# Attention of a small transformer stack: value and output weights folded per head, probabilities turned on VectorE, products on four row groups

## The reference

```python
def attn_layer(x, Wqkv, qs, ksc, Wo):          # x: 16 x 256 x 128; 16 heads of 64; float32
    q, k, v = jnp.split(x @ Wqkv, 3, -1)       # each to (b, head, token, 64)
    q = l2norm(q) * qs; k = l2norm(k) * ksc
    q = q * cos * scale + rotate_half(q) * sin * scale
    k = k * cos * inv + rotate_half(k) * sin * inv
    out = local_attention(q, k, v)             # windows of 32 queries, 64 keys each: its own and the one before
    return out.transpose(0, 2, 1, 3).reshape(b, n, INNER) @ Wo

for i in range(6):
    x = attn_layer(shift_tokens(x), Wqkv[i], q_scale[i], k_scale[i], Wo[i]) + x
    x = ffn_layer(shift_tokens(x), ln_g[i], ln_b[i], W1[i], b1[i], W2[i], b2[i]) + x
```

## Time and profile before

| | us |
|---|---|
| median of 3 runs | 3451.17 (3447.96 to 3452.07) |
| the profiled execution | 3446.72 |
| its span | 3444.9 |
| PE busy, share of the span | 96% |
| ACT, DVE, POOL busy, shares | 79%, 71%, 42% |
| mean share of the 16 DMA engines, q1 | 52.5% |

### The profile page before, as it was taken

One profiled execution on the slowest core, in us unless ns is written; L12 is line 12 of the kernel. 1 busy time (PEld: TensorE's weight loads), 2 busy tenths in 40 slices (PEclk: granted clock), 3 DMA queues, 4 the chain that ended last, 5 costly groups with the idle time before them and its releaser, 6 DMA issues.

```text
span 3444.9 us, 152307 instructions
## 1 busy us (share of the span) xinstructions
PE 3317.0 (96%) x63036; PEld 2464.0 (72%) x63228; DVE 2439.2 (71%) x5141; ACT 2709.1 (79%) x9033; POOL 1444.9 (42%) x1276
## 2 busy tenths in 40 slices
PE   6789999999999999999999999999999999999997
PEld 4457777777777777777777777777777777777775
DVE  5667777777777777777777777777777777777774
ACT  5667887878788787778787887878878787878876
POOL 2244443544444354444354444444434354444431
PEclk9999999999999999999999999999999999999999
DMA  2045555555655555555555555565565556455553
GB/s 73 1 109 130 134 122 127 134 132 121 145 117 124 132 134 131 125 134 119 126 140 120 135 129 131 119 145 118 124 137 119 131 132 140 113 129 126 117 135 83
DMA packets 360553, 421.42 MB, mean 122 GB/s; under 512 B 51571, under 2 KB 265094, under 8 KB 359094
## 3 DMA queue, kind: packets, MB, share of 16 engines
q1 hardware_dynamic: 359862, 411.67, 52.5%
HBM read 19.30 MB, written 2.10 MB: 6 GB/s over the span
## 4 chain that ended last, share of the span: by engine, by line
PE 71%; POOL 17%; issue 4%; DVE 2%; ACT 1%; DMA 0%; SPq 0%; POOLq 0%; DVEq 0%
PE ring_ps L1227 16%; POOL qs L610 12%; PE out_ps L1319 12%; PE out_ps L1329 10%; PE ring_ps L1272 8%; PE small_ps L1238 6%; PE score_ps L1290 5%; PE ring_ps L1301 4%; PE ring_ps L1365 4%; POOL probs L594 3%; DVE prod L986 2%; PE ring_ps L1262 2%; PE out_ps L1343 2%; PE score_ps L1282 1%; PE small_ps L1246 1%
## 5 line engine op out<-in xcount | busy, mean ns | idle before, releaser
L767 ACT ACTIVATE probs<-score_ps,neg_max,rq 128x64 f32<-128x64 f32 x3072 | 1200.5, 421 | 94.6 <-DVE neg_max L1024 93.4
L986 DVE TENSOR_TENSOR prod<-ring_ps,tables 128x512 f32<-128x512 f32 x1536 | 957.7, 681 | 288.8 <-PE ring_ps L1227 255.9
L610 POOL TENSOR_TENSOR ks<-prod 128x1024 f32<-128x1024 f32 x192 | 452.7, 2358 | 861.2 <-DVE prod L986 861.2
L1227 PE MATMUL ring_ps<-xs,wqk 128*128 128x256 f32 x3072 | 768.4, 388 | 17.9 <-issue 12.8
L767 ACT ACTIVATION_READ_ACCUMULATOR probs<-score_ps,neg_max,rq 128x1 f32 x3072 | 679.0, 221 | 0.0
L723 ACT ACTIVATE square<-ring_ps,biases 128x512 f32<-128x512 f32 x768 | 517.8, 688 | 198.8 <-DVE prod L986 197.0
L1227 PEld LDWEIGHTS ring_ps<-xs,wqk 128*128 128x128 f32 x3072 | 570.6, 191 | 107.9 <-issue 20.3
L594 POOL TENSOR_TENSOR probs<-probs,inv_sums 128x512 f32<-128x512 f32 x384 | 400.8, 1044 | 581.2 <-DVE inv_sums L1038 581.1
L610 POOL TENSOR_TENSOR qs<-prod 128x1024 f32<-128x1024 f32 x192 | 453.7, 2363 | 382.8 <-DVE prod L986 382.8
L1319 PEld LDWEIGHTS out_ps<-pt,v 64*64 64x64 f32 x24576 | 395.3, 135 | 113.7 <-issue 111.5
L756 ACT ACTIVATE att_t<-out_ps 128x512 f32<-128x512 f32 x384 | 217.3, 592 | 295.6 <-PE out_ps L1319 295.5
(11 more groups left out here) (182 smaller groups left out, 3791.5 us busy)
## 6 DMA issues: line engine op xcount, KB each, us to landing
v<-vs SPq DMA_DIRECT2D x1344, 128.0 KB
qt<-qs SPq DMA_DIRECT2D x768, 128.0 KB
kt<-ks SPq DMA_DIRECT2D x768, 128.0 KB
v<-vs SPq DMA_DIRECT2D x192, 64.0 KB
wqk<-in_L_ffn_Wqkv SPq DMA_DIRECT2D x6, 1024.0 KB, 5.1
wv<-in_L_ffn_Wqkv SPq DMA_DIRECT2D x6, 512.0 KB, 5.7
wo<-in_L_ffn_Wo SPq DMA_DIRECT2D x6, 512.0 KB
out_dram<-ks SPq DMA_DIRECT2D x16, 128.0 KB, 1.9
```

The costliest lines, as they stand in the source:

```text
L610: pool.tensor_tensor(dst, prod_a[p % 2], prod_b[p % 2], ALU.add).then_inc(rot_ready, 1)
L767: last = nc.scalar.activation(probs[i][:, j, e, :], score_ps[e][:, KEYS * j:KEYS * (j + 1)], ACT.Exp, bias=neg_max[:, h:h + 1], scale=rq[p ...
L986: last = V.tensor_tensor((prod_b if a else prod_a)[p % 2][:, f, :] .rearrange("p (u c) -> p u c", u=2), bank[:, :].rearrange("p (u c) -> p ...
L1227: last = mm(bank_of(s)[:, TOKENS * f:TOKENS * (f + 1)], wqk[:, n, 2 * c + f, a, :], xs[:, WINDOW:PADDED], start=True, stop=True)
```

## The change

- The values are not computed any more. For each head, the value weights (128 x 64) and its output weights (64 x 128) are multiplied on the chip into one 128 x 128 matrix, `fold`. That is done for layer 0 before the first batch, in four parts, and for the layer after in four parts (MW on PE, MC on ACT) in the batches 8 to 11 of a layer. The steps V, VC, the moves MV and the load of `wv` go.
- In place of the values the shifted input itself is turned (XT, four transposes on PE; XC, a copy on DVE) into `x2`, in two versions 32 tokens apart, for the keys of the window before and of the own window.
- The probabilities are turned in blocks of 32 x 32 by `V.transpose` on DVE (DT, four instructions of 128 x 512), in place of T and TC.
- PV0 and PV1: eight products each, with 32 contracted rows, 128 output rows and 512 columns (16 heads by 32 queries); the four windows of a tile lie on four row groups and write to four banks. The step before had 64 products in two halves, on 64 x 64.
- The output of PV is 16 heads by 128 channels, so that WO has 16 products in place of 8. It is cut in four steps, WO0 to WO3. The copies OC are eight of 128 x 512, five on ACT and three on DVE.
- The banks are five, given by a table `BANK_OF`, and `bank_free` waits for whoever last used each bank. The orders of all engines are new; S0 stands first on PE. MQ and MK stay, behind the same semaphores, as do all steps not named here.
- `wv_turned` is an input laid out by the host in place of the columns of V.

```diff
 PE_ORDER = """
-PA0 PB0 PA1 S00 S01 PB1 BI WO PA2 NK CEN PB2 VAR PA3 PB3 TK UP0 UP1 S10 S11 V0 UP2 T00 TU NQ KN0 PAD V1 PV00 KN1
-TQ T01 V2 DN T10 PV01 V3 T11 PV10 PV11
+S0 PB0 PA0 PB1 WO0 PA1 WO1 PA2 PB2 PA3 NK S1 TK WO2 PB3 BI WO3 TU XT CEN KN1 VAR NQ KN0 UP0 UP1 TQ UP2 PV0 DN PV1
+MW
 """
 DVE_ORDER = """
-XS RA0 RB0 RA1 M0 RB1 BI XA XB AR00 RA2 RB2 CK XG RB3 RA3 H0 M1 AR01 H1 TC00 UC H2 KM0 CQ VC1 KM1 AR10 TC01 X
-AR11 TC10 VC3 TC11
+XS M0 RA0 RB0 RB1 AR00 RA1 RA2 RB2 RA3 CK DT00 M1 RB3 BI XA XB AR10 AR01 UC XC KM1 XG KM0 CQ DT01 AR11 H0 H1 DT11
+DT10 H2 OC00 OC03 X OC12
 """
 ACT_ORDER = """
-QA0 QB0 QA1 E00 QB1 E01 E02 SQ QA2 LN E03 QB2 RTK LG G0 QB3 QA3 G1 VC0 G2 LE E10 E11 E12 E13 VC2 OC00 OC01 OC10
-RTQ OC11
+E00 E01 QA0 QB0 QB1 E02 QA1 E03 QA2 QB2 RTK QA3 E10 E11 E12 SQ QB3 LN E13 LG G0 G1 G2 LE OC02 OC01 RTQ OC11 OC13
+OC10 MC
 """
 POOL_ORDER = """
-AD0 AD1 TB0 AD2 AN00 AD3 RK AN01 TB1 AN10 AN11
+AD0 AN00 AD1 TB0 AD2 RK AD3 TB1 AN01 AN11 AN10
 """
 SP_ORDER = """
-LK MQ MK LV LL MV
+LK MQ MK LL LM
+"""
+BANK_OF = """
+PB0:3 PA0:4 PB1:2 WO0:0 PA1:1 PA2:3 PB2:2 PA3:4 PB3:2 TU:1 XT:3 CEN:4 KN1:0 KN0:1 UP0:3 UP1:0 UP2:2 PV0:4,0,3,1
+DN:2 PV1:1,0,3,4 BI:4 MW:3,4
 """
...
-            def move_v():
-                for e in range(2):
-                    for m in range(WPT):
-                        src = vs[WINDOW * m:WINDOW * (m + 1), :, e, :]
-                        for half in range(2):
-                            row_ = KEYS * e + WINDOW * half
-                            w0_ = m + 1 - half
-                            tiles = TILES if w0_ < WPT else TILES - 1
-                            sp.dma_start(v2[row_:row_ + WINDOW, w0_:w0_ + WPT * (tiles - 1) + 1:WPT, :],
-                                         src[:, 0:tiles, :]).then_inc(v_moved, 16)
...
+            def make_fold(layer, part, banks):
+                if part == 0:
+                    pe.wait_ge(fold_landed, 32 * (layer + 1))
+                for j in range(2):
+                    for e in range(2):
+                        side = slice(64 * e, 64 * e + 64)
+                        last = mm(banks[e][:, DIM * j:DIM * (j + 1)], wv_turned[side, 2 * part + j, :],
+                                  wo[side, 2 * part + j, :], start=True, stop=True, skip_group_check=True)
+                last.then_inc(fold_made, 1)
...
+                if kind == "XT":
+                    pe.wait_ge(xs_ready, at(g, 1, 1))
                     bank_free(g, s)
...
+                    for k in range(2):
+                        for i in range(TILES):
+                            col = P * i + WINDOW * k
+                            last = pe.transpose(bank_of(s)[:, P * (TILES * k + i):P * (TILES * k + i + 1)],
+                                                xs[:, col:col + P], ident[:, :])
+                    last.then_inc(x_turned, 1)
...
+                if kind == "PV":
+                    i = s[1]
+                    pe.wait_ge(x2_ready, at(g, 1, 1))
                     bank_free(g, s)
...
+                    last_turn = max(rank(DVE_ORDER, ("DT", i, c), "DT") for c in range(2))
+                    pe.wait_ge(turn_ready, at(g, 2 * TILES, last_turn + 1))
+                    for k in range(2):
                         for w in range(WPT):
+                            rows = slice(WINDOW * w, WINDOW * (w + 1))
+                            last = mm(bank_of(s, w), x2[rows, parity, k, i, :],
+                                      turned[rows, i, :, WINDOW * k:WINDOW * (k + 1)],
+                                      start=(k == 0), stop=(k == 1))
+                    last.then_inc(pv_ready, 1)
                 if kind == "WO":
...
+                    part = s[1]
+                    if part == 0:
+                        bank_free(g, s)
+                        for order in (ACT_ORDER, DVE_ORDER):
+                            copied(pe, copies(order)[-1], g)
+                        if b == 0:
+                            pe.wait_ge(fold_ready, 2 * M_PARTS * (layer + 1))
+                    for h in range(WO_PARTS * part, WO_PARTS * (part + 1)):
+                        last = mm(bank_of(("WO", 0)), fold[layer % 2][:, h, :], att_t[:, h, :], start=(h == 0),
+                                  stop=(h == HEADS - 1))
+                    if part == WO_PARTS - 1:
+                        last.then_inc(wo_ready, 1)
+                if kind == "MW" and runs(s, g):
+                    bank_free(g, s)
+                    make_fold(layer + 1, b - M_FIRST, [bank_of(s, e) for e in range(2)])
                 if kind == "BI" and b == 0:
                     pe.wait_ge(late_landed, layer * (16 * late_per_layer) + 16 * late_per_layer)
...
+                if kind == "DT":
                     i, c = s[1], s[2]
...
+                    dve.wait_ge(scaled, at(g, 2 * TILES, rank(POOL_ORDER, ("AN", i, c), "AN") + 1))
+                    if g > 0:
+                        dve.wait_ge(pv_ready, at(g - 1, TILES, rank(PE_ORDER, ("PV", i), "PV") + 1))
+                    V.transpose(turned[:, i, 8 * c:8 * c + 8, :].rearrange("p h k -> p (h k)"),
+                                probs[i][:, 4 * c:4 * c + 4, :, :].rearrange("p j e k -> p (j e k)")
+                                ).then_inc(turn_ready, 1)
+                if kind == "OC":
+                    i, w = s[1], s[2]
+                    dve.wait_ge(pv_ready, at(g, TILES, rank(PE_ORDER, ("PV", i), "PV") + 1))
+                    dve.wait_ge(wo_ready, at(g, 1))
+                    V.tensor_copy(att_t[:, :, P * i + WINDOW * w:P * i + WINDOW * (w + 1)],
+                                  bank_of(("PV", i), w).rearrange("p (h q) -> p h q", q=WINDOW)
+                                  ).then_inc(o_dve, 1)
```

More of the change, by code:

```diff
@@ L111, in rank, with runs, copies @@
     return [x for x in order if x[0] in kinds].index(s)
-RING = [s for s in PE_ORDER if s[0] in ("PA", "PB", "TU", "KN", "V", "T", "DN", "PAD")]
-BANKS = 3
-assert len(RING) % BANKS == 0
+def runs(s, g):
+    b, layer = g % BATCH, g // BATCH
+    if s[0] == "BI":
+        return b == 0
+    if s[0] in ("MW", "MC"):
+        return layer < DEPTH - 1 and M_FIRST <= b < M_FIRST + M_PARTS
+    return True
+def copies(order):
+    return [x for x in order if x[0] == "OC"]
+BANKS = 5
+HALF_BANK = ("WO", "CEN", "DN", "TU", "BI", "MW")
 def build(nc, t):
@@ L149, in build @@
         wqk = sb("wqk", [P, 2, QUADS, 2, P])
-        wv = sb("wv", [P, INNER])
-        wo = [sb(f"wo{i}", [P, PAIRS, DIM]) for i in range(2)]
+        wv_turned = sb("wv_turned", [P, PAIRS, DIM])
+        wo = sb("wo", [P, PAIRS, DIM])
+        fold = [sb(f"fold{i}", [P, HEADS, DIM]) for i in range(2)]
         w1 = [sb(f"w1_{i}", [P, 2 * DIM_INNER]) for i in range(2)]
@@ L353, in walk, with users_before @@
                         step(s, g, b, g % 2, layer)
-        def users_before(seq, s, g, banks):
-            k = seq.index(s) - banks
-            while k >= -2 * len(seq):
-                u = seq[k % len(seq)]
-                gu = g + (stage(u) - stage(s) + k // len(seq))
-                if 0 <= gu < DEPTH * BATCH:
-                    yield u, gu
-                k -= banks
-        def user_before(seq, s, g, banks):
-            return next((x for x in users_before(seq, s, g, banks) if x[0] != ("PAD",)), (None, None))
+        def users_before(s, g):
+            need = set(BANK_OF[s])
+            period, k = g - stage(s), PE_ORDER.index(s)
+            while need and period >= -1:
+                k -= 1
+                if k < 0:
+                    k, period = len(PE_ORDER) - 1, period - 1
+                u = PE_ORDER[k]
+                gu = period + stage(u)
+                if u in BANK_OF and 0 <= gu < DEPTH * BATCH and runs(u, gu):
+                    for i, bank in enumerate(BANK_OF[u]):
+                        if bank in need:
+                            need.remove(bank)
+                            yield u, i, gu
         def walk_first(order, step):
@@ L712, in first_step, with copy_fold @@
                                          bias=mod[:, b, 3:4], scale=mod[:, b, 4:5]).then_inc(lh[1], 1)
+            def copy_fold(layer, part, banks):
+                for e in range(2):
+                    heads = fold[layer % 2][:, :, :].rearrange("p (j e) n -> p j e n", e=2)
+                    nc.scalar.activation(heads[:, 2 * part:2 * part + 2, e, :],
+                                         banks[e].rearrange("p (j n) -> p j n", n=DIM), ACT.Copy
+                                         ).then_inc(fold_ready, 1)
             walk_first(ACT_FIRST, first_step)
+            for part in range(M_PARTS):
+                act.wait_ge(fold_made, part + 1)
+                copy_fold(0, part, [bank_ps[n][:, 0:TOKENS] for n in ((0, 1), (2, 4))[part % 2]])
             def step(s, g, b, parity, layer):
@@ L1216, in step @@
+            first_proj = next(x for x in PE_ORDER if x[0] in ("PA", "PB"))
+            first_kn = next(x for x in PE_ORDER if x[0] == "KN")
```

(1 more changed line is left out.)

336 lines of the change are left out of this document (156 added, 180 removed).

## The result

The changed kernel takes 3556.31 us (median of 4 runs, 3550.04 to 3558.44), the kernel before 3451.62 beside it: 1.0302 times as long, 95% interval 1.0284 to 1.032. The profiled execution has a span of 3548.2. So it is slower by 3.0%, where 2.6% was forecast (3540).

What follows compares the result with a forecast made beforehand. The prediction took PE to bound the kernel before, and the chain of q's and k's moves to bound it after: 96 x 34.3 + 245 = 3538, plus 2 outside the span, 3540 us (+2.6%), range 3410 to 3650.

Steps and rivals of the forecast that it cites:

- The deciding chain: From k's landing through scores, projections and POOL's last sum to SP's moves of q and k: 34.3 us a batch.
- the walk: Step-by-step sum along the move chain, using durations from the trace before: POOL's last sum ends at 20.6, period 34.3 us.
- One sign: On PE ahead of S0's scores: idle time put down to k's DMA, 1.5 to 3 us a period.
- The second chain: From ACT's exponentials to the second gelu, then PV0, bank copies, PV1, scores and masks: 32.4 us a batch.
- E00: First part of the exponentials on ACT, where the second chain starts; from it to the second gelu 23.1 us was walked.
- TensorE's sum: PE's busy time per batch: 33.1 - 10.1 + 3.5 + 0.5 + 3.7 + 0.1 = 30.8 us.
- Row groups: In PV0 and PV1 on PE: four row groups run at once, 1.8 us a step, 3.7 for both.
- the third rival: Chain of ACT, DVE and PV takes over, transposes at 1.35, row groups half overlapping: period about 36, 3700 us; chance 0.10.
- The fourth rival: Row groups on PE don't overlap: both PV steps 6.9 us, period 42.6, 4330 us; chance 0.05.
- The fold: 20 small steps in all, under 0.2 us a period, plus four before the first batch, some 5 us once.
- The moves are shorter: SP's 16 issues of q and k take 10.3 us with V off the queue: period 33.0, 3415 to 3450; chance 0.20.
- PE stays the bound: TensorE takes the whole gain, the moves costing no wait: 30.8 x 96 + 260 = 3215 us; chance 0.10.

Runs made afterwards that it cites:

- e1: The changed kernel with four of the eight DMAs of every move of q left out behind the first batch: 3488.70 us, ratio 1.0129.
- e2: The changed kernel with one swap in PE_ORDER, PB3 before WO2, everything computed: 3491.63 us, ratio 1.0133.
- e4: The changed kernel with four of the eight DMAs of every move of q and of k left out behind the first batch: 3487.61 us, ratio 1.0126.
- e9: The changed kernel, orders laid anew, 28 steps allowed one period earlier, first scores ahead of PV1, everything computed: 3348.87 us, ratio 0.9712.
- e6: The changed kernel with PB3 before WO2, MW between UP0 and UP1 in other banks, and MC ahead of the first gelu: 3454.78 us, ratio 1.0015.
- e5: The changed kernel with all steps kept, the five engine orders and the bank table laid afresh: 3666.80 us, ratio 1.0626.

## Why the prediction was right, and where it was off

**The deciding chain: right, in its place and its size.** AD3 ended 20.85 behind the scores (median; 20.6 in the walk), MQ followed by 0.1, MK stood directly behind MQ. From the first issue to the landing it took 13.2 (median; 12.2 to 14.1), where the walk had 11.6 + 1.9 = 13.5. The two terms are not separate: in the mean the whole took 13.0 behind the 38 bursts whose 16 issues took under 10.7, and 13.1 behind the 56 longer ones, since k often landed later behind a short burst. One of them, SP's rows:

```profile
1844.62 5.11 SPq L503 DMA_DIRECT2D qt<-qs  x8
1849.85 5.10 SPq L503 DMA_DIRECT2D kt<-ks  x8
```

The last issue ends at 1854.95; the scores start at 1858.00, 3.05 later. In 65 of 94 batches the scores start 0.04 behind k's landing; 20 of the 29 others are those with a fold step. e1, e2 and e4 show that the moves did decide: each of three ways to shorten that chain gives the same 65 to 69 us. One sign failed all the same: the idle time ahead of S0 was to be 1.5 to 3 us a batch and was 1.0 where there was any, and in total no more than PV's. PE's waits in total thus put the two chains level; that the scores start right behind k's landing, and the experiments, decide between them.

**The second chain: right in its path, mis-sized.** Walked at 32.4, measured at 33.2. Its terms: E00 to G1 23.4 for 23.1; PV0 to PV1 3.60 for 3.4, since DN stands between them and takes 1.67 with its change of tiling; PV1 to the scores 2.46 for 2.0, since a PV step takes 1.93 to the next start where 1.83 was walked, and the two masks 0.53 where 0.2 was; G1 to PV0 0.6 for 0.5. These, each short by 0.1 to 0.5, are 1.1 us; the 0.3 kept for steps between engines goes off, which leaves 0.8. It did not spoil the forecast, for 34.3 stood above both; it spoiled the expectations of e1, e4 and e2, which counted with 1.9 us of room below the move chain where there were some 1.2 (medians 34.3 and 33.2, batches without a fold step).

**TensorE's sum: the direction right, 0.7 short.** Predicted 30.8 a batch, measured 31.5 in the kernel after (each product from its start to the next start, mean of 21 ordinary batches; the kernel before gives 33.0 in that way). What was removed was right: 10.2 for 10.1. Of what was added, WO has 3.6 for 3.5, XT 0.66 for 0.5, the two PV steps 3.93 for 3.7. The rest, 0.5, lies in steps that the change does not touch: DN 1.56 for 1.30, CEN and VAR 1.33 for 0.97, KN 0.78 for 0.64, against 0.3 less in the projections. What differs is what stands behind them: a step of another tiling or one that waits, where in the kernel before mostly a step of the same tiling followed. DN shows it best: before PV1 (32*128) it takes 1.56, in e9, where S0's masks (128*128) follow, 1.29 (1657.83 to 1659.12), and 1.30 in the kernel before.

**Row groups: right.** The groups by line of the kernel after, PV's products and DVE's transposes:

```profile
L1373 PE MATMUL bank_ps<-turned,x 32*128 32x512 f32 x3072 | 385.6, 614 | 77.9 <-DVE hidden L1104 64.6 <-issue 3.9 <-DVE att_t L1063 1.6
...
L1056 DVE STREAM_TRANSPOSE turned<-probs 128x512 f32<-128x512 f32 x384 | 269.7, 703 | 7.1 <-POOL probs L607 2.9
```

A PV step takes 1.93 where 6.9 would be needed one after another: 3.6 times, with the 0.1 of the change of tiling taken off 3.8 times. The 3.07 of the Trainium skill (TensorE: Matmul & The Clock Gate, section "Measured speedup vs the span model") would have given 2.2 by the prediction's estimate; the trace is nearer to four. The transposes take 0.70 for 0.68, so the bound of 1.35, and with it the third rival, falls. The fourth rival (no overlap) falls too.

**The fold: wrong.** It was priced at its products, under 0.2 us a batch in the mean, and its waits at nothing. Its products are that small. Its place is not: once the moves are out of the way the 20 batches lose 1.8 us each, 36 us in all (e2 against e6). The failed step is that a moved or added step was priced by its engine's time and not by what it waits for (PV1's copies) and who stands behind it (S0, on both chains). In the kernel after part of this is covered by the wait for k, and 1.2 us a fold batch are left.

**The rivals.** "The moves are shorter" had the bound of 10.3. Bursts of that length came, but k landed later behind them and the batch shown took 34.4; and with half of the moves the second chain and the fold still hold the time at 3488 (e4). Its 3415 was out of reach. "PE stays the bound" came true, but only in e9 and at 31.9 a batch, not 30.8: 3349, not 3215.

**The sum.** 96 x 34.3 + 245 had to meet 3548. The batches without a fold step took 34.35 in the mean, as walked; the 20 with one took 35.5, and that makes the mean 34.6 (195.3 to 3481.5, over 95) and adds 23 us. What lies around the batches is 18 shorter than the 245 (3548.2 - 96 x 34.6 = 227). That the forecast came within 0.5% is thus in part luck: the fold's waits, which it had at nothing, and the part around, which it had too long, nearly cancel, and so do AD3, 0.25 too early, and the moves, 0.3 too long.

## What to carry to other kernels

When a change takes work off the engine that is full, walk every chain that closes from one period to the next before counting the gain, and list them in order of length: what the first gives back is only its distance to the second. Price a moved step by whose buffers it takes and who stands behind it, not by its duration. And when several new orders end at the same time with the engine 4% idle, look at which steps could run a period earlier: that gained 2.9% here, where none of the orders tried within the period was faster than the kernel before.

## What the runs showed of the hardware that I had not expected

- A VectorE operation of 0.17 us with both inputs in SBUF took 1.79 us beside a GpSimd sum of 2.35 us: it ended with the sum. Transposes and PSUM copies did not change (0.70 and 0.69 us).
- After TensorE had stood idle for 1.59 us its granted clock was 0.54 in the stretch behind (1837.30 to 1840.70 of e5), mostly the lower of its levels, 1.2 GHz, and its products there took nearly twice as long (1.94 for 1.07). Batches of e5 in which the clock fell took 36.04 us, those with the same late maximum and the full clock 35.05.
- Small products took longer where a step of another tiling followed: six passes of DN took 1.67 us from start to start between two PV steps in e2, and 1.29 ahead of S0's masks in e9, where 1.30 is six times the 0.216 of a pass.
- In the kernel after, eight moves of q and eight of k in a row were issued in 10.3 to 12.0 us, but a shorter burst did not land sooner: from first issue to last landing it was 13.0 us in the mean where the issues took under 10.7, and 13.1 where they took longer.
